# Bilinear products stored with the slice index innermost, GRU weights loaded at the start of the attention, head sums by block

## The chip, the cores and the metric
The kernel runs on one core of a Trainium2 chip. The metric is device time in microseconds of one execution: 2214.73 us is the median of three runs (2214.09 to 2214.98) of the kernel before.

## The reference
Four layers over x (4096 nodes x 128 features) and adj (4096 x 4096, sparse in values, dense in storage), each on the layer norm h of the running x. Cut to what matters here:

```python
# L0 gnn: 3 attention heads, then two GRU cells
node_support = adj_without_diagonal @ h
edge_support = mean over heads of softmax(att) * adj_without_diagonal @ (h @ W[i])
edge_output = gru(node_support, h, edge weights)
node_output = gru(edge_support, h, node weights)
x = x + diag[:, None] * (edge_output + node_output)
# L0 ffn: 1 shared + 8 routed experts, top 2
# L1 gnn (bilinear): K = 16 slices
node = h @ W1                                # 4096 x 16
hw = einsum('nc,kcf->nkf', h, W2)            # 4096 x 16 x 128
X = einsum('nk,nkf->nf', node, hw)           # sum over the 16 slices
x = x + relu(adj @ X + node @ b)
# L1 ffn: 8 routed experts, top 2
```

## The kernel before, in words
Five engines run queues of their own (SP issues all DMAs), written out by hand and tied together by counting semaphores; no planner stands behind them. The stages follow one another: layer norm, a pass over adj that counts signs and edges, softmax denominators, tables T of the heads, attention, GRU, layer norm, FFN 0, layer norm, bilinear stage, adjacency product, layer norm, FFN 1.

Attention: four blocks of 1024 output nodes (rb), each a loop over 32 tiles n of 128 adj rows. Per tile SP loads Ab (line 352) and Tt (355); GpSimd clears the diagonal where it lies in the tile (449) and raises a_prep; ScalarE makes three sigmoids ss (589) and the bf16 copy Ahi (599); VectorE makes Alo (1268), ph (1271) and pl (1274); TensorE does 24 matmuls (876) into the eight PSUM banks: heads 0 to 2 and the node support. Between blocks, after the first tile of the new block has been prepared, `evacuate` empties the banks: ScalarE copies nsT and head 2 (603, 604), VectorE multiplies each head by the reciprocal RD (1282 twice, 1285) and raises es_out. Ahead of it all SP stores the reciprocals to DRAM and waits for that store (342, 343). After the last block SP loads gruW, gruB and dB, the diagonal in every partition (366 to 368), with one semaphore g_in; GpSimd adds the three heads for all eight chunks of 512 nodes (456 to 460); VectorE (1297), TensorE (889) and GpSimd (462) wait for all three loads. VectorE then makes the bias sums gbr (1299) and releases TensorE through g_nin.

GRU: 16 groups (8 chunks, two cells s) of 12 fp32 matmuls (900 to 905), gates on ScalarE (623, 625, 630), products on VectorE (1308 to 1320), scaling by dB and the addition into xT on GpSimd (470, 474).

Bilinear stage: 32 tiles n of 128 nodes, buffers s = n % 2. TensorE makes h @ W2 for all 16 slices into four banks (12 matmuls, 986). Each slice is scaled by its node value: slices 0 to 7 by eight ScalarE copies (710), slices 8 to 15 by one VectorE product (1441). GpSimd adds the two halves of the slices (487, prod into halves), VectorE sums the remaining eight (1449, xf) and casts to bf16 (1452, Xb[0]), GpSimd makes the rest Xb[1] (493). TensorE's tile n+2 waits for the two products of n (983, 984), these for the halving of n-2 (b_half), the halving for both products of its own tile.

Of the kernel before, what the change touches and what calls it, by code (L numbers as in the profile page):

```python
# [56 lines left out]
def build(nc, a, out):  # L57
    with ExitStack() as ctx:
# [107 lines left out]
        nsT = sb("nsT", [P, N], F32, 184)  # L166
        dB = sb("dB", [P, N], F32, 104)

        gruW = sb("gruW", [P, 4, 3 * P], F32, 32)
        gruB = sb("gruB", [P, 4, 3], F32, 39)  # L170
        gbr = sb("gbr", [P, 2, 2], F32, 39.5)
        gR = [sb(f"gR{i}", [P, CH], F32, 40 + 2 * i) for i in range(2)]
        gZ = [sb(f"gZ{i}", [P, CH], F32, 44 + 2 * i) for i in range(2)]
        gM = [sb(f"gM{i}", [P, CH], F32, 48 + 2 * i) for i in range(2)]
        gU = [sb(f"gU{i}", [P, CH], F32, 52 + 2 * i) for i in range(2)]

        Wr = sb("Wr", [P, NE], F32, 56)
        rb2 = sb("rb2", [P, 2, NE], F32, 56.25)
        lg = sb("lg", [P, NT, NE], F32, 57)
        rq = sb("rq", [P, NT, NE], F32, 58)  # L180
        s1 = sb("s1", [P, NT, NE], F32, 59)
# [19 lines left out]
        bb = sb("bb", [K1, P], F32, 81.5)  # L201
        wb = sb("wb", [P, P], F32, 82)
        h3b = [sb(f"h3b{i}", [P, N], BF16, 84 + 8 * i) for i in range(2)]
        prod = [sb(f"prod{i}", [P, K1, P], F32, 100 + 8 * i) for i in range(2)]
        nodek = sb("nodek", [P, NT, K1], F32, 116)
        xf = [sb(f"xf{i}", [P, P], F32, 118 + .5 * i) for i in range(2)]
        halves = [sb(f"halves{i}", [P, K1 // 2, P], F32, 119 + 4 * i) for i in range(2)]
        Xb = [sb(f"Xb{i}", [P, NT, P], BF16, 48 + 8 * i) for i in range(2)]
        A4 = [sb(f"A4{i}", [P, N], F32, kb) for i, kb in enumerate((128, 144, 32, 64))]
        A4hi = [sb(f"A4hi{i}", [P, N], BF16, kb) for i, kb in enumerate((160, 168, 84, 92))]  # L210
# [69 lines left out]
        def _(sp):  # L280
# [82 lines left out]
            sp.wait_ge(a_lo, NRB * nsign * NT + AS)  # L363
            sp.dma_start(xT[:, :], a["xT"]).then_inc(x_in, 16)
            sp.wait_ge(es_out, HEADS * NRB + 1)
            sp.dma_start(gruW[:, :, :], a["gruW"]).then_inc(g_in, 16)
            sp.dma_start(gruB[:, :, :], a["gruB"]).then_inc(g_in, 16)
            sp.dma_start(dB[:, :], diag_d.partition_broadcast(P)).then_inc(g_in, 16)

            def ffn_loads(k, nE, nF):  # L370
                if k == 1:
# [51 lines left out]
        @block.gpsimd  # L423
        def _(pool):

            pool.wait_ge(range_l, 1)
            pool.partition_all_reduce(sm[:, 3:6], sm[:, 0:3], P, ROP.max).then_inc(range_g, 1)
            pool.wait_ge(range_l, 2)
            pool.partition_all_reduce(sm[:, 7:8], sm[:, 6:7], P, ROP.max).then_inc(range_g, 1)

            pool.wait_ge(th_hi, 1)
            pool.tensor_tensor(gwb[1][:, :], gw[:, :], gwb[0][:, :], ALU.subtract).then_inc(th_lo, 1)
            pool.wait_ge(th_hi, 2)
            pool.tensor_tensor(hTs[1][:, :], hT[:, :], hTs[0][:, :], ALU.subtract).then_inc(th_lo, 1)
            pool.wait_ge(nsign_ok, 1)
            nsign = pool.value_load(nsg[0:1, 0:1], min_val=1, max_val=2)

            for rb in range(NRB):
                with pool.Fori(0, nsign) as sg:
                    for lo, hi in ((0, rb * TPB), (rb * TPB, rb * TPB + TPB), (rb * TPB + TPB, NT)):  # L440
                        if lo == hi:
                            continue
                        with pool.Fori(lo // AS, hi // AS) as i:
                            for s in range(AS):
                                n = (rb * nsign + sg) * NT + AS * i + s
                                pool.wait_ge(a_in[s], ((rb * nsign + sg) * (NT // AS) + i) * 32 + 32)
# [8 lines left out]
            pool.wait_ge(es_out, HEADS * NRB + 1)
            for q in range(NC):
                c = slice(q * CH, (q + 1) * CH)
                pool.tensor_tensor(esT[:, c], esT[:, c], esP[:, 1, c], ALU.add).then_inc(es_add, 1)
                pool.wait_ge(es_add, q + 1)
                pool.tensor_tensor(esT[:, c], esT[:, c], esP[:, 2, c], ALU.add).then_inc(es_ok, 1)  # L460

            pool.wait_ge(g_in, 48)
            pool.wait_ge(x_in, 32)
            pool.sem_inc(g_used, 2)
            with pool.Fori(0, NC) as q:
                for s in range(2):
                    n = 2 * q + s
                    pool.wait_ge(g_new, n + 3)
                    pool.sem_inc(seen, 1)
                    pool.tensor_tensor(gU[s][:, :], gU[s][:, :], dB[:, nlast(q)], ALU.mult).then_inc(g_scaled, 1)  # L470
                    pool.wait_ge(g_scaled, n + 1)
                    pool.wait_ge(g_used, n + 2)
                    pool.sem_inc(seen, 1)
                    pool.tensor_tensor(xT[:, nlast(q)], xT[:, nlast(q)], gU[s][:, :], ALU.add).then_inc(g_used, 1)

            def bilinear_weights():
                pool.wait_ge(b_hi, 1)
                pool.tensor_tensor(bw2[1][:, :], bw2f[:, :], bw2[0][:, :], ALU.subtract).then_inc(b_w_lo, 1)
                pool.wait_ge(b_hi, 2)
                pool.tensor_tensor(bw1b[1][:, :], bw1[:, :], bw1b[0][:, :], ALU.subtract).then_inc(b_w_lo, 1)  # L480

            bilinear_weights()
            def halve(n, s):
                pool.wait_ge(b_prod_a, n + 3)
                pool.wait_ge(b_prod_d, n + 3)
                pool.wait_ge(b_sum, n + 1)
                pool.tensor_tensor(halves[s][:, :, :], prod[s][:, 0:K1 // 2, :], prod[s][:, K1 // 2:, :],  # L487
                                   ALU.add).then_inc(b_half, 1)
# [46 lines left out]
        def _(act):  # L535
# [165 lines left out]

            act.wait_ge(b_node_ok, 1)
            act.sem_inc(b_prod_a, 2)
            with act.Fori(0, NT // 2) as i:
                for s in range(2):
                    n = 2 * i + s
                    act.wait_ge(b_ps, n + 1)
                    act.wait_ge(b_half, n + 1)
                    for k in range(K1 // 2):
                        last = nc.scalar.activation(  # L710
                            prod[s][:, k, :], psum[:, 4 * s + k // 4, k % 4 * P:k % 4 * P + P], ACT.Copy,
                            scale=nodek[:, ds(n, 1), k:k + 1].rearrange("p o k -> p (o k)"))
                    last.then_inc(b_prod_a, 1)
# [46 lines left out]
        def _(pe):  # L760
# [256 lines left out]
        def _(dve):  # L1017
# [535 lines left out]
```

## Time and profile before
| | |
|---|---|
| median of 3 runs | 2214.73 us |
| profiled execution | 2213.51 us |
| its span | 2211.7 us |
| mean granted TensorE clock | 0.906 of full |
| TensorE / VectorE / ScalarE / GpSimd busy | 82% / 77% / 63% / 8% |

A row of a timeline is: start in us, duration in us, engine, line, operation, out<-in, xcount of merged instructions; in brackets how long the engine was idle before it and what released it. SPq, DVEq and the like are sequencers, PEld is TensorE's weight load.

### The profile page before, as it was taken

The page shows a single profiled execution, that of the slowest core. Times are in us where ns is not written, and L with a number is a line of the kernel's source. Part 1 is how long each engine was busy: PE and PEld are TensorE (multiplying, and loading weights), DVE is VectorE, ACT ScalarE, POOL GpSimd, SP SyncE. Part 2 cuts the span into 40 slices and gives each one's busy share as a digit, 9 for nine tenths or more (in the row PEclk, how much of TensorE's full clock was granted, in tenths as well). Part 3 has the DMA queues.
Part 4 walks back from the last instruction along what each step waited for, and adds up shares of the span by engine and source line. Part 5 has one row for each costly group of instructions (what it writes and reads, how often), then busy time and mean ns, then how long its engine had stood idle before and what let it go on. Part 6 is the DMA issues. An engine that isn't in the chain of part 4 may idle for free.

```text
span 2211.7 us, 30420 instructions
## 1 busy us (share of the span) xinstructions
PE 1821.4 (82%) x8950; PEld 875.2 (40%) x9101; DVE 1692.5 (77%) x1792; ACT 1398.9 (63%) x1767; POOL 187.9 (8%) x154
## 2 busy tenths in 40 slices
PE   4221573799999999999798899999987789997997
PEld 4111221344444444444345444444452234463332
DVE  4555427788898888888467688888859988855898
ACT  1777006778787787788334566776645567626885
POOL 0000001100000000000442000000017710000000
PEclk7555788899999999999897899999989999988999
DMA  5997025454545544554600311232030079814532
GB/s 166 429 427 319 0 80 205 162 155 150 170 150 156 169 148 154 170 151 149 238 0 0 79 38 39 48 60 45 1 123 11 0 305 429 366 39 81 98 89 76
DMA packets 79575, 313.89 MB, mean 142 GB/s; under 512 B 13958, under 2 KB 14438, under 8 KB 69494
## 3 DMA queue, kind: packets, MB, share of 16 engines
q1 hardware_dynamic: 79500, 312.98, 42.5%
q8 instruction: 36, 0.59, 0.1%
q14 instruction: 39, 0.32, 0.1%
HBM read 297.88 MB, written 15.08 MB: 142 GB/s over the span
## 4 chain that ended last, share of the span: by engine, by line
PE 40%; DVE 9%; POOL 3%; issue 3%; ACT 1%; DMA 1%; DVEq 0%; SPq 0%; POOLq 0%; ACTq 0%
PE psum L926 9%; PE psum L936 8%; PE psum L1008 7%; PE psum L876 7%; POOL halves L487 3%; DVE hidp L1382 2%; DVE xT L1404 2%; DVE yT L1401 2%; DVE prod L1441 2%; PE psum L900 1%; PE psum L902 1%; PE psum L748 1%; PE psum L914 1%; PE psum L743 1%; PE psum L754 1%
## 5 line engine op out<-in xcount | busy, mean ns | idle before, releaser
L589 ACT ACTIVATE ss<-KR,dpt 128x1024 bf16<-128x1024 int16 x384 | 413.1, 1138 | 112.0 <-DVE pl L1274 111.2
L876 PE MATMUL psum<-ph,Tt 128*128 128x512 bf16 x1502 | 411.9, 380 | 8.8 <-DVE pl L1274 7.0
L665 ACT ACTIVATE hid<-psum,fB 128x512 f32<-128x512 f32 x416 | 271.2, 686 | 151.2 <-PE psum L926 108.0
L936 PE MATMUL psum<-hidp,fW 128*128 128x512 bf16 x1215 | 289.2, 381 | 23.3 <-DVE hidp L1382 17.3
L926 PE MATMUL psum<-hTp,fW 128*128 (+1 forms) x1224 | 295.3, 384 | 5.9 <-ACT mk L679 2.8
L1382 DVE TENSOR_TENSOR hidp<-hid,hidp 128x512 bf16<-128x512 f32 x416 | 268.7, 687 | 26.7 <-DVE xT L1404 10.4
L1271 DVE TENSOR_TENSOR ph<-ss,Ahi 128x3072 bf16<-128x3072 bf16 x128 | 225.2, 1760 | 61.9 <-PE psum L876 60.2
L876 PE MATMUL psum<-pl,Tt 128*128 128x512 bf16 x752 | 225.9, 380 | 0.8
L876 PEld LDWEIGHTS psum<-ph,Tt 128*128 128x128 bf16 x1536 | 150.5, 98 | 190.4 <-issue 6.4
L1274 DVE TENSOR_TENSOR pl<-ss,Alo 128x3072 bf16<-128x3072 bf16 x128 | 224.2, 1751 | 0.0
L936 PEld LDWEIGHTS psum<-hidp,fW 128*128 128x128 bf16 x1248 | 117.6, 98 | 183.2 <-issue 42.1
L926 PEld LDWEIGHTS psum<-hTp,fW 128*128 128x128 bf16 x1248 | 123.2, 99 | 155.1 <-issue 12.1
L1268 DVE TENSOR_TENSOR Alo<-Ab,Ahi 128x1024 bf16<-128x1024 f32 x128 | 163.2, 1275 | 17.3 <-ACT Ahi L599 17.3
L876 PE MATMUL psum<-Ahi,Tt 128*128 128x512 bf16 x503 | 151.0, 380 | 24.2 <-DVE Alo L1268 20.3
L659 ACT ACTIVATE hidp<-hid 128x512 bf16<-128x512 f32 x272 | 163.4, 624 | 0.0
L1468 DVE TENSOR_TENSOR A4lo<-A,A4hi 128x4096 bf16<-128x4096 f32 x32 | 141.3, 4425 | 21.5 <-ACT A4hi L719 21.5
L541 ACT ACTIVATE Ar<-Ar 128x4096 f32<-128x4096 f32 x32 | 115.7, 3617 | 58.2 <-DVE keep L1102 58.2
L719 ACT ACTIVATE A4hi<-A 128x4096 bf16<-128x4096 f32 x32 | 115.4, 3616 | 50.0 <-PE psum L1008 23.2
L599 ACT ACTIVATE Ahi<-Ab 128x1024 bf16<-128x1024 f32 x128 | 133.3, 1042 | 6.4 <-issue 6.3
L785 PE MATMUL psum<-uvs,keep 128*128 128x18 bf16 x1024 | 32.7, 176 | 122.0 <-DVE keep L1102 122.0
L1008 PE MATMUL psum<-A4hi,Xb 128*128 128x512 bf16 x512 | 115.9, 379 | 0.0
L986 PE MATMUL psum<-bw,h3b 128*128 128x512 bf16 x368 | 86.1, 385 | 34.2 <-DVE prod L1441 32.5
(228 smaller groups left out, 2110.6 us busy)
## 6 DMA issues: line engine op xcount, KB each, us to landing
Ar<-in_adjT SPq DMA_DIRECT2D x32, 2048.0 KB, 12.9
Ab<-in_adjT SPq DMA_DIRECT2D x128, 512.0 KB, 4.1
A<-in_adjT SPq DMA_DIRECT2D x32, 2048.0 KB, 11.1
Tt<-T_d SPq DMA_DIRECT2D x128, 256.0 KB, 2.6
mB<-mk_d SPq DMA_DIRECT2D x128, 256.0 KB, 7.6
T_d<-tb SPq DMA_DIRECT2D x32, 256.0 KB, 2.0
RD<-rden_d SPq DMA_DIRECT2D x12, 512.0 KB, 5.3
fWs<-in_W SPq DMA_DIRECT2D x2, 2304.0 KB, 16.5
```

The lines of the kernel that those rows point to most:

```text
L589: last = nc.scalar.activation(ss[s % 2][:, h, :], KR[:, h, rb * RB:(rb + 1) * RB], ACT.Sigmoid, scale=STEP, bias=dpt[:, ds(t * HEADS + h, 1)])
L659: nc.scalar.activation(hidp[j % ring][:, 0, :], hid[j % HB][:, :], ACT.Copy).then_inc(hid_hi[k], 1)
L665: nc.scalar.activation(hid[j % HB][:, :], psum[:, j % HB, :], func, bias=fB1[:, j:j + 1]).then_inc(act_done[k], 1)
L876: last = nc.tensor.matmul(psum[:, 2 * h + q, :], Tt[s % AS][:, h, w, :], mv[:, q * CH:(q + 1) * CH], start=fresh and k == 0, stop=False, s ...
L926: last = nc.tensor.matmul(psum[:, j % HB, :], fW[0][x][:, j * P:(j + 1) * P], hTp[y][:, nlast(q)], start=(w == 0), stop=(w == 2))
L936: last = nc.tensor.matmul(psum[:, HB + e % dn, :], fW[1][x][:, j * P:(j + 1) * P], hidp[j % ring][:, y, :], start=(f == 0 and w == 0), sto ...
L1008: last = nc.tensor.matmul(psum[:, q, :], Xb[w][:, ds(n, 1), :].rearrange("p o f -> p (o f)"), mv[s][:, q * CH:(q + 1) * CH], start=False, ...
L1268: V.tensor_tensor(Alo[s % AS][:, :], Ab[s % AS][:, :], Ahi[s % AS][:, :], ALU.subtract).then_inc(a_lo, 1)
L1271: V.tensor_tensor(ph[s % 2][:, :, :], ss[s % 2][:, :, :], Ahi[s % AS][:, :].unsqueeze(1).to_broadcast([P, HEADS, RB]), ALU.mult).then_inc( ...
L1274: V.tensor_tensor(pl[s % 2][:, :, :], ss[s % 2][:, :, :], Alo[s % AS][:, :].unsqueeze(1).to_broadcast([P, HEADS, RB]), ALU.mult).then_inc( ...
L1382: V.tensor_tensor(hidp[j % ring][:, 1, :], hid[j % HB][:, :], hidp[j % ring][:, 0, :], ALU.subtract).then_inc(hid_lo[k], 1)
L1468: V.tensor_tensor(A4lo[s][:, :], A4[s][:, :], A4hi[s][:, :], ALU.subtract).then_inc(l_lo, 1)
```

## The change
Three edits.
1. SP issues gruW and gruB after the tables are stored and before it waits for the reciprocals; gruW, gruB, gbr, Wr and rb2 move to other addresses. dB stays behind the last evacuation and is counted on x_in, for which only GpSimd waits; TensorE waits for g_in 32 and es_out 12 instead of 48 and 13, VectorE for g_in 32.
2. GpSimd's head sums become a function for two chunks, called for block rb-1 behind the loop of block rb, and for the last block behind that.
3. prod and halves are laid out [128, 128, 16] and [128, 128, 8], the slice innermost. ScalarE's copies write one slice of it each (steps of 16 elements), VectorE's product writes through a rearranged pattern, the reduction reads contiguous memory. The cast Xb[0]<-xf goes from VectorE to ScalarE, behind the scaled copies of tile n+2.

```diff
-            sp.dma_start(gruW[:, :, :], a["gruW"]).then_inc(g_in, 16)      # behind es_out 13
-            sp.dma_start(gruB[:, :, :], a["gruB"]).then_inc(g_in, 16)
-            sp.dma_start(dB[:, :], diag_d.partition_broadcast(P)).then_inc(g_in, 16)
+            sp.dma_start(dB[:, :], diag_d.partition_broadcast(P)).then_inc(x_in, 16)
...
+            sp.dma_start(gruW[:, :, :], a["gruW"]).then_inc(g_in, 16)      # ahead of rden_ok
+            sp.dma_start(gruB[:, :, :], a["gruB"]).then_inc(g_in, 16)
             sp.wait_ge(rden_ok, 1)
...
+            def head_sums(rb):
+                pool.wait_ge(es_out, HEADS * rb + HEADS + 1)
+                for q in range(rb * RB // CH, (rb + 1) * RB // CH):
+                    c = slice(q * CH, (q + 1) * CH)
+                    pool.tensor_tensor(esT[:, c], esT[:, c], esP[:, 1, c], ALU.add).then_inc(es_add, 1)
+                    pool.wait_ge(es_add, q + 1)
+                    pool.tensor_tensor(esT[:, c], esT[:, c], esP[:, 2, c], ALU.add).then_inc(es_ok, 1)
...
+                if rb > 0:
+                    head_sums(rb - 1)
+            head_sums(NRB - 1)
+            pool.wait_ge(x_in, 48)
...
-                pool.tensor_tensor(halves[s][:, :, :], prod[s][:, 0:K1 // 2, :], prod[s][:, K1 // 2:, :],
+                pool.tensor_tensor(halves[s][:, :, :], prod[s][:, :, 0:K1 // 2], prod[s][:, :, K1 // 2:],
...
+            scaled_products(0, 0)
+            scaled_products(1, 1)
+            with act.Fori(0, NT // 2 - 1) as i:
                 for s in range(2):
+                    scaled_products(2 * i + s + 2, s)   # 8 copies into prod[s][:, :, k]
+                    high_x(2 * i + s, s)                # waits b_sum, casts xf into Xb[0]
+            high_x(NT - 2, 0)
+            high_x(NT - 1, 1)
...
-                V.tensor_tensor(prod[s][:, K1 // 2:, :],
+                V.tensor_tensor(prod[s][:, :, K1 // 2:].rearrange("p f k -> p k f"),
...
-                V.tensor_reduce(xf[s][:, :], halves[s][:, :, :].rearrange("p k f -> p f k"), AX,
-                                ALU.add).then_inc(b_sum, 1)
-                dve.wait_ge(b_sum, n + 3)
-                V.tensor_copy(Xb[0][:, ds(n, 1), :].rearrange("p o f -> p (o f)"), xf[s][:, :]).then_inc(b_x_hi, 1)
+                V.tensor_reduce(xf[s][:, :], halves[s][:, :, :], AX, ALU.add).then_inc(b_sum, 1)
```

## Rows read from the trace of the kernel before

**Rows 1.** The page's chain that ended last, by line.
```profile
PE psum L926 9%; PE psum L936 8%; PE psum L1008 7%; PE psum L876 7%; POOL halves L487 3%; DVE hidp L1382 2%; DVE xT L1404 2%; DVE yT L1401 2%; DVE prod L1441 2%; PE psum L900 1%; PE psum L902 1%; PE psum L748 1%; PE psum L914 1%; PE psum L743 1%; PE psum L754 1%
```
**Rows 2.** Timeline, from attention to GRU.
```profile
1082.80 1.22 DVE L1285 TENSOR_TENSOR esP<-esP,RD 128x1024 f32<-128x1024 f32 x1
...
1093.38 1.07 DVE L1299 TENSOR_TENSOR gbr<-gruB 128x2 f32<-128x2 f32 x2 [9.37 <-DMA dB<-diag_d]
...
1093.69 2.07 PE L900 MATMUL psum<-nsT,gruW 128*128 x2 [13.21 <-DVEq L1301]
...
1101.14 0.69 ACT L623 ACTIVATE gR<-psum,gbr 128x512 f32<-128x512 f32 x1 [18.68 <-PE psum L905]
...
1106.24 0.69 ACT L623 ACTIVATE gR<-psum,gbr 128x512 f32<-128x512 f32 x1 [3.84 <-PE psum L905]
```
**Rows 3.** A stretch: us, then PE, PEld, DVE, ACT, POOL busy (x), clock, DMA share, GB/s.
```profile
1080.00:1093.00 13.00, 0.49 (x3) 0.00 (x0) 3.49 (x3) 1.94 (x2) 8.67 (x7) 0.65 0.60 223
```
**Rows 4.** Timeline, start of the attention.
```profile
388.92 0.35 SPq L342 DMA_DIRECT2D rden_d<-den  x1
...
391.22 0.37 SPq L352 DMA_DIRECT2D Ab<-in_adjT  x1
...
399.10 1.01 PE L876 MATMUL psum<-Ahi,Tt 128*128 128x512 bf16 x2 [17.89 <-DVE Alo L1268]
```
**Rows 5.** DMA issues, 1060 to 1200: count, KB each, us to landing.
```profile
gruW<-in_gruW SPq DMA_DIRECT2D x1, 768.0 KB, 4.1
```
**Rows 6.** Timeline, VectorE and GpSimd at once in the last GRU updates.
```profile
1183.49 1.48 POOL L470 TENSOR_TENSOR gU<-gU,dB 128x512 f32<-128x512 f32 x1 [2.54 <-DVE gU L1320]
...
1183.87 1.65 DVE L1319 TENSOR_TENSOR gU<-gU,gZ 128x512 f32<-128x512 f32 x1
```
**Rows 7.** Timeline, border of attention blocks 1 and 2.
```profile
726.30 1.04 ACT L599 ACTIVATE Ahi<-Ab 128x1024 bf16<-128x1024 f32 x1
...
731.60 1.06 ACT L599 ACTIVATE Ahi<-Ab 128x1024 bf16<-128x1024 f32 x1
731.64 1.75 DVE L1274 TENSOR_TENSOR pl<-ss,Alo 128x3072 bf16<-128x3072 bf16 x1
...
740.25 2.35 DVE L1282 TENSOR_TENSOR esP<-psum,RD 128x1024 f32<-128x1024 f32 x2 [1.75 <-PE psum L876]
...
750.89 0.60 PE L876 MATMUL psum<-ph,Tt 128*128 128x512 bf16 x2 [1.87 <-DVE pl L1274]
```
**Rows 8.** Instructions grouped by line: busy us, mean ns, idle before.
```profile
L460 POOL TENSOR_TENSOR esP<-esP 128x512 f32<-128x512 f32 x8 | 10.1, 1263 | 0.6
L493 POOL TENSOR_TENSOR Xb<-xf,Xb 128x128 f32 x30 | 12.8, 426 | 8.3 <-DVE Xb L1452 8.3
L1449 DVE TENSOR_REDUCE xf<-halves 128x128 f32<-128x1024 f32 x32 | 61.7, 1928 | 0.8 <-POOL halves L487 0.8
L1353 DVE TENSOR_REDUCE rs<-rq 128x32 f32<-128x256 f32 x4 | 1.7, 420 | 0.1
L710 ACT ACTIVATE prod<-psum,nodek 128x128 f32<-128x128 f32 x256 | 69.5, 383 | 57.8 <-PE psum L986 57.8
```
**Rows 9.** Tile halves, its writer: duration ns min/median/max, first and last start.
```profile
L487 POOL TENSOR_TENSOR halves<-prod x32: 2348/2355/2364, 1657.2 to 1774.1; 128x1024 f32<-128x1024 f32 x32
```
**Rows 10.** Timeline, one beat of the bilinear stage and its last cast.
```profile
1663.70 2.35 POOL L487 TENSOR_TENSOR halves<-prod 128x1024 f32<-128x1024 f32 x1 [0.72 <-DVE prod L1441]
...
1665.47 0.67 DVE L1452 CAST Xb<-xf 128x128 f32 x1
1666.10 1.23 DVE L1441 TENSOR_TENSOR prod<-psum,nodek 128x1024 f32<-128x1024 f32 x1
...
1667.54 2.36 POOL L487 TENSOR_TENSOR halves<-prod 128x1024 f32<-128x1024 f32 x1 [0.78 <-DVE prod L1441]
...
1766.60 2.76 PE L986 MATMUL psum<-bw,h3b 128*128 128x512 bf16 x12 [1.06 <-DVE prod L1441]
...
1778.35 0.23 DVE L1452 CAST Xb<-xf 128x128 bf16<-128x128 f32 x1
```

More of the change, by code:

```diff
@@ L167, in build @@
         dB = sb("dB", [P, N], F32, 104)
-        gruW = sb("gruW", [P, 4, 3 * P], F32, 32)
-        gruB = sb("gruB", [P, 4, 3], F32, 39)
-        gbr = sb("gbr", [P, 2, 2], F32, 39.5)
+        gruW = sb("gruW", [P, 4, 3 * P], F32, 56)
+        gruB = sb("gruB", [P, 4, 3], F32, 62)
+        gbr = sb("gbr", [P, 2, 2], F32, 62.125)
         gR = [sb(f"gR{i}", [P, CH], F32, 40 + 2 * i) for i in range(2)]
@@ L175, in build @@
         gU = [sb(f"gU{i}", [P, CH], F32, 52 + 2 * i) for i in range(2)]
-        Wr = sb("Wr", [P, NE], F32, 56)
-        rb2 = sb("rb2", [P, 2, NE], F32, 56.25)
+        Wr = sb("Wr", [P, NE], F32, 62.25)
+        rb2 = sb("rb2", [P, 2, NE], F32, 62.5)
         lg = sb("lg", [P, NT, NE], F32, 57)
@@ L203, in build @@
         h3b = [sb(f"h3b{i}", [P, N], BF16, 84 + 8 * i) for i in range(2)]
-        prod = [sb(f"prod{i}", [P, K1, P], F32, 100 + 8 * i) for i in range(2)]
+        prod = [sb(f"prod{i}", [P, P, K1], F32, 100 + 8 * i) for i in range(2)]
         nodek = sb("nodek", [P, NT, K1], F32, 116)
         xf = [sb(f"xf{i}", [P, P], F32, 118 + .5 * i) for i in range(2)]
-        halves = [sb(f"halves{i}", [P, K1 // 2, P], F32, 119 + 4 * i) for i in range(2)]
+        halves = [sb(f"halves{i}", [P, P, K1 // 2], F32, 119 + 4 * i) for i in range(2)]
         Xb = [sb(f"Xb{i}", [P, NT, P], BF16, 48 + 8 * i) for i in range(2)]
@@ L452, in _ @@
                                 pool.wait_ge(a_hi, n + 1)
[L455 to L463, printed above, removed]
+                if rb > 0:
+                    head_sums(rb - 1)
+            head_sums(NRB - 1)
+            pool.wait_ge(x_in, 48)
             pool.sem_inc(g_used, 2)
@@ L703, in _, with scaled_products, high_x @@
             act.sem_inc(b_prod_a, 2)
-            with act.Fori(0, NT // 2) as i:
-                for s in range(2):
[L706 to L713, printed above, removed]
+            def scaled_products(n, s):
+                act.wait_ge(b_ps, n + 1)
+                act.wait_ge(b_half, n + 1)
+                for k in range(K1 // 2):
+                    last = nc.scalar.activation(
+                        prod[s][:, :, k], psum[:, 4 * s + k // 4, k % 4 * P:k % 4 * P + P], ACT.Copy,
+                        scale=nodek[:, ds(n, 1), k:k + 1].rearrange("p o k -> p (o k)"))
+                last.then_inc(b_prod_a, 1)
+            def high_x(n, s):
+                act.wait_ge(b_sum, n + 3)
+                nc.scalar.activation(Xb[0][:, ds(n, 1), :].rearrange("p o f -> p (o f)"), xf[s][:, :],
+                                     ACT.Copy).then_inc(b_x_hi, 1)
+            scaled_products(0, 0)
+            scaled_products(1, 1)
+            with act.Fori(0, NT // 2 - 1) as i:
+                for s in range(2):
+                    scaled_products(2 * i + s + 2, s)
+                    high_x(2 * i + s, s)
+            high_x(NT - 2, 0)
+            high_x(NT - 1, 1)
             act.wait_ge(b_x, NT + 2)
@@ L886, in _ @@
                         attend(rb, m, s)
-            pe.wait_ge(g_in, 48)
+            pe.wait_ge(g_in, 32)
             pe.wait_ge(ns_out, 2 * NRB)
-            pe.wait_ge(es_out, HEADS * NRB + 1)
+            pe.wait_ge(es_out, HEADS * NRB)
             with pe.Fori(0, NC) as q:
@@ L1295, in _ @@
             evacuate(NRB - 1)
-            dve.wait_ge(g_in, 48)
+            dve.wait_ge(g_in, 32)
             for s in range(2):
```

## The prediction
> **What bounds the kernel now.** I read the chain of waits first. By line it is TensorE for most of the span (FFN lines 926 and 936, the adjacency product 1008, attention 876), but one GpSimd line stands among them, 487, with VectorE's 1441 beside it [rows 1]: the bilinear stage is bound off TensorE. Two places then matter. In the hand-over from attention to GRU the last head is scaled at 1082.80 to 1084.02; then VectorE's little bias sum waits 9.37 us for the diagonal broadcast dB to land and TensorE stands 13.21 us until 1093.69 [rows 2]. In the bilinear stage a tile takes (1774.1 - 1657.2)/31 = 3.77 us [rows 9]. Its beat is in the timeline [rows 10]: VectorE's product ends at 1667.33, GpSimd's halving starts 0.21 later and takes 2.36, and VectorE, done with its reduction, cannot finish the bf16 cast before the halving ends: it starts at 1665.47, lasts until 1666.14 while the halving ended at 1666.05, and the same cast takes 0.23 when GpSimd is idle [last row of rows 10]. Only then does the next product start. Product 1.2 + hop 0.2 + halving 2.36 = 3.8. TensorE waits 1.06 us a tile for the product; its 12 matmuls of (2.76 - 0.38)/11 = 0.216 need 2.6.
>
> **Part 1: GRU start.** TensorE and VectorE no longer wait for dB, only for gruW and gruB, here in SBUF since the attention began. What is late next is VectorE's queue: gbr stands behind the last scaling, which ends at 1084.02, so TensorE starts at about 1084.0 instead of 1093.69: -9.7. It could be 1083.2, since at 1093 TensorE was released 0.31 after the first gbr instruction began, before the pair was done [rows 2]: VectorE's sequencer runs ahead. dB now lands some 9 us after 1084, as before; its first reader is GpSimd's scaling of the first update, which VectorE makes behind the second group's gates, and these came 1106.24 - 1093.69 = 12.5 us after TensorE's start (10 at full clock), so it stays hidden. In-block sums of the last block (4 instructions of 1.26, [rows 8]) end by 1089 and are wanted in the seventh chunk, tens of us later.
> Clock: the first group of matmuls took 1101.14 - 1093.69 = 7.4 us against 1106.24 - 1101.14 = 5.1 for the next [rows 2], because the granted clock had dropped from the 2.4 GHz level to the 1.2 GHz one: its mean over the gap is 0.65 [rows 3]. A mean of 0.65 over 1080 to 1093 at levels 1 and 0.5 puts the fall near 1084, just where TensorE will start. So between 0 and 2.2 us comes back; I take the middle, -1.1.
>
> **Part 2: the GRU loads' new place.** SP now issues gruW and gruB after the last table store and ahead of the 48 KB store of the reciprocals, whose completion gates the adjacency loads, and these TensorE's first matmul (399.10, after 17.89 us idle) [rows 4]. The store was issued at 388.92, the instant its predecessors had landed, and the first load at 391.22. Two issues of 0.35 to 0.45 come first: at least +0.8. The 768 KB transfer needs 4.1 us to land [rows 5] and goes through the same queue ahead of the store: if the store lands just behind it, the first load moves from 391.2 to about 393.4, +2.2; at most +4.3, the whole landing after both issues. I take +2.2. Attention runs at TensorE's pace from there, so nothing hides it.
>
> **Part 3: head sums by block.** Block 0 and 1's sums now stand in GpSimd's queue between two blocks: 4 instructions, and behind them the next block's a_prep, which ScalarE's Ahi needs, then Alo, ph, pl, VectorE's evacuation, and so TensorE's second head. The price depends on who has the SBUF port. At 1183.49 a GpSimd sum began, and the VectorE product begun at 1183.87 took 1.65 instead of 0.69, ending 0.55 after GpSimd [rows 6]: one waits for the whole of the other. The Trainium skill's "SBUF — State Buffer", section "SBUF: two separate sides", says just this: the port pair DVE and GpSimd share is an exclusive lock held for a whole instruction. By that rule the trace agrees, and nothing in the sum changes.
> At the border of blocks 1 and 2 GpSimd would start after Ahi at 727.3, get the port when VectorE's running instruction ends a microsecond later, and then alternate with Alo, ph and pl: 728.2 + 4 x 1.15 + the three of 1.2, 1.7 and 1.7 between them less their overlaps gives about 737.2 for the end of the fourth sum, where a_prep came at once before. Ahi moves from 731.60 to 737.3, Alo to 738.4, ph 739.6, pl 741.3, and the evacuation from 740.25 to 743.0 [rows 7]. The current block's last pl ends at 736.0 instead of 733.4 and is wanted 18 matmuls of 0.216 before the block's end at 740.1, at 736.2. TensorE's first head of the new block is 1.6 late, but on the tile behind it TensorE already waited 1.87 us for pl (at 750.89), which takes most of this up. I take +0.25 for each of two borders, +0.5; none below, and 3 each (the evacuation's delay, unabsorbed) above: 0 to +6. The sums of block 2 run beside attention's last tile, for which VectorE has finished early.
>
> **Part 4: bilinear stage.** Per tile:
> - The reduction reads contiguous memory. The same operation with the same run of eight, 256 elements, takes 0.42 [rows 8]; at 1.04 ns an element (one per VectorE cycle) 1024 take 1.21 instead of 1.93. The old one read in steps of 512 bytes, so a step costs 0.72/1024 = 0.7 ns an element on reading.
> - The product now writes in steps of 64 bytes. No strided write of that size is in the trace. Bounds: free (1.22), or twice the reading surcharge (2.65). I take the one row that shows a surcharge: 1.22 + 0.7 = 1.92. VectorE's tile is then 1.92 + 1.21 - 0.1 of overlap = 3.05.
> - ScalarE's eight copies (69.5/32 = 2.17 a tile, [rows 8]) write in the same steps: free, or 128 x 0.7 ns = 0.09 each, 2.9 for eight; twice that 3.6. I take 2.9. The cast is added: between the copies' pitch (2.17 - 0.38)/7 = 0.26 and their length 0.38, 0.3.
> - GpSimd reads two runs of eight in every sixteen and writes contiguously: I take 2.36 unchanged; bounds below.
> The tile's pace is the longest of: TensorE 2.6; VectorE 3.05; ScalarE 2.9 + 0.3 = 3.2; GpSimd 2.36 + 0.43 + 0.1 = 2.9; and the ring over two tiles, halving 2.36, hop 0.2, copies 2.9, cast 0.35, hop 0.2, split 0.43, hop 0.1 = 6.5, or 3.25 a tile. Gain (3.77 - 3.25) x 31 = -16.1.
> At the tail the last reduction is 0.65 shorter and the cast before the wb copy is gone (0.15): -0.8. The adjacency product behind it is TensorE's own and only moves; its first three tiles are loaded long before.
> The Trainium skill's "SBUF — State Buffer", section "Specifications (TRN2)", speaks against the layout: lines are 16 bytes, and each access that crosses to a new line pays unless a line is hit twice. By it the writes pay as the reads did; the case without it is the first rival. No run here shows a write yet.
>
> **The sum.** -9.7 - 1.1 + 2.2 + 0.5 - 16.1 - 0.8 = -25.0. The profiled execution took 2213.51 (span 2211.7): 2188.5. The median of the runs is 1.2 above it, so about 2189.
>
> **Rivals.**
> 1. Strided writes are free. Copies 2.17: ring 5.8/2 = 2.9, GpSimd 2.9; pace 2.95, gain 25.4, time 2189 - 9.3 = about 2180. [...] Against: the surcharge seen on reads.
> 2. Writes cost twice that. VectorE 2.65 + 1.21 - 0.1 = 3.76, ring with copies of 3.6 also 3.6: no gain in the loop, and only parts 1 to 3 and the tail (-8.9) stand: about 2206.
> 3. Slower than before: GpSimd restarts on every run of eight. Its elements cost (2.355 - 0.426)/896 = 2.15 ns [rows 8, 9]. A restart worth eight elements, 17 ns x 128 = 2.2, makes the halving 4.56 and the pace 5.1: +41 - 9 = +32, 2247. It decides from a halving of 3.5, that is a restart of 4.3 elements, where it eats the 8.9 of the other parts. For it: GpSimd is the engine next in line in the ring and has no row with short runs. Against: its plain rows scale strictly with elements.
> The Trainium skill's "GPSIMD Engine Reference", section "Performance pitfalls for Q7 kernels", gives a surcharge of half for reads whose step exceeds 8 bytes; the innermost step here is 4, so by its letter the halving stays. Counted as strided it would be 3.5, just the point where the gain is gone.
> 4. The change does not do what it says: the GRU start is held by something else (the sums, es_ok, ScalarE's evacuation). Against it: of the waits, only those for VectorE's two evacuations and ScalarE's copies can be as late as 1084, and the sums of the first blocks lie inside the attention.
>
> **Chances.** Forecast (pace 3.1 to 3.45) 0.48, its own range 2182 to 2196; rival 1 0.24; paces between the forecast and rival 2 0.15; rival 3 0.10, most of it slower; rival 4 or an attention that loses all its 6 us 0.03. The range 2175 to 2206 leaves out rival 3 and little else. Within 0.2% (4.4 us, about what a measurement of this kernel tells from no change) only a halving near 3.5 lands. Faster 0.87, same 0.03, slower 0.10.
>
> **What would show it.** The wait before the first GRU matmul at 3 to 4 us instead of 13; the first adjacency load about 4.5 us behind the reciprocals' predecessors; Alo beside GpSimd's sums at 2.3 at two borders; the reduction at 1.21, the product near 1.9, the copies' pitch near 0.35, the halving 2.36, 31 tiles 3.25 apart. Wrong if the halving is not 2.36, or if the product stays at 1.22.

## The result, and the profile after

The changed kernel takes 2176.12 us (median of four executions, 2174.39 to 2179.8) against 2214.47 (2214.09 to 2214.98) of four executions of the kernel before, taken beside it: a ratio of 0.9829, 95% interval 0.9812 to 0.9846, or 38 us less. 2189 was forecast, with a range of 2175 to 2206. The profiled execution took 2179.80 (span 2178.0, granted clock 0.906).

| stage, in the profiled executions | before | after | difference |
|---|---|---|---|
| up to the store of the last table | 388.92 | 393.14 | +4.2 |
| from there to the first attention matmul | 10.18 | 13.10 | +2.9 |
| attention | 681.43 | 680.36 | -1.1 |
| end of attention to the first layer norm matmul on xT | 97.6 | 86.8 | -10.8 |
| bilinear stage: first weight load of line 986, now 1003, to the first matmul of 997, now 1014 | 128.6 | 100.9 | -27.7 |
| all the rest | | | -1.2 |
| sum | | | -33.7 |

The first row is work that the change does not touch. Over the profiled executions of all ten kernels of this document it runs from 388.9 to 396.1, and the kernel before has the lowest. Without that row the sum is -37.9, near the 38.35 between the medians; but the profiled execution of the changed kernel was also the slowest of its four, 3.7 above their median, so the agreement is partly chance (see Open).

The chain of the page, by line, has lost GpSimd's halving (3% in [rows 1]); VectorE's product has fallen from 2% to 1%, and TensorE's own 1003 stands in their place.
```profile
PE psum L943 9%; PE psum L953 9%; PE psum L1025 8%; PE psum L893 7%; DVE hidp L1399 2%; PE psum L1003 2%; DVE xT L1421 2%; DVE yT L1418 2%; PE psum L917 1%; PE psum L919 1%; PE psum L765 1%; PE psum L931 1%; DVE prod L1458 1%; PE psum L760 1%; PE psum L771 1%
```
Timeline of the changed kernel, start of the attention (answers to [rows 4]).
```profile
393.14 0.35 SPq L341 DMA_DIRECT2D gruW<-in_gruW  x1
393.55 0.42 SPq L342 DMA_DIRECT2D gruB<-in_gruB  x1
394.01 0.43 SPq L344 DMA_DIRECT2D rden_d<-den  x1
398.57 0.35 SPq L354 DMA_DIRECT2D Ab<-in_adjT  x1
...
406.24 1.01 PE L893 MATMUL psum<-Ahi,Tt 128*128 128x512 bf16 x2 [20.82 <-DVE Alo L1285]
```
The reciprocals' store goes out 0.87 later than it could, and then needs 4.56 until the first load instead of 2.30.

Timeline from attention to GRU, and the granted clock (column 7) of the 13 us that answer to [rows 2, 3]; the whole kernel runs 6 us later here, so the stretch starts at 1086.
```profile
1086.60 2.36 DVE L1299 TENSOR_TENSOR esP<-psum,RD 128x1024 f32<-128x1024 f32 x2 [4.37 <-PE psum L893]
1088.87 1.22 DVE L1302 TENSOR_TENSOR esP<-esP,RD 128x1024 f32<-128x1024 f32 x1
1089.40 2.07 PE L917 MATMUL psum<-nsT,gruW 128*128 x2 [2.84 <-DVE esP L1299]
1090.00 0.22 DVE L1316 TENSOR_TENSOR gbr<-gruB 128x2 f32<-128x2 f32 x2
1090.11 0.33 SPq L368 DMA_DIRECT2D dB<-diag_d  x1
...
1096.37 0.69 ACT L627 ACTIVATE gR<-psum,gbr 128x512 f32<-128x512 f32 x1 [7.83 <-PE psum L922]
```
```profile
1086.00:1099.00 13.00, 10.16 (x22) 4.42 (x21) 4.84 (x7) 3.20 (x4) 5.01 (x4) 0.87 0.51 196
```
TensorE waits 2.84 us instead of 13.21, and not even for gbr: the first matmul starts at 1089.40, the bias sum at 1090.00.

Timeline of the border of blocks 1 and 2 (answers to [rows 7]): GpSimd's four sums alternate with VectorE's two-input operations, and each is stretched by the other.
```profile
733.78 1.62 POOL L442 TENSOR_TENSOR esP<-esP 128x512 f32<-128x512 f32 x1 [87.25 <-ACT Ahi L603]
734.20 2.29 DVE L1285 TENSOR_TENSOR Alo<-Ab,Ahi 128x1024 bf16<-128x1024 f32 x1
...
736.41 2.82 DVE L1288 TENSOR_TENSOR ph<-ss,Ahi 128x3072 bf16<-128x3072 bf16 x1
...
739.15 2.81 DVE L1291 TENSOR_TENSOR pl<-ss,Alo 128x3072 bf16<-128x3072 bf16 x1
...
740.43 2.66 POOL L444 TENSOR_TENSOR esP<-esP 128x512 f32<-128x512 f32 x1
...
740.89 1.06 ACT L603 ACTIVATE Ahi<-Ab 128x1024 bf16<-128x1024 f32 x1 [3.35 <-issue]
...
746.32 1.02 ACT L607 ACTIVATE nsT<-psum 128x1024 f32<-128x1024 f32 x1 [4.38 <-PE psum L893]
```
The bilinear stage: groups by line (answers to [rows 8]; busy us, mean ns, idle before), tile halves ([rows 9]), and one beat ([rows 10]).
```profile
L491 POOL TENSOR_TENSOR halves<-prod 128x1024 f32<-128x1024 f32 x32 | 75.6, 2364 | 16.3 <-ACT prod L713 15.7
L713 ACT ACTIVATE prod<-psum,nodek 128x128 f32<-128x128 f32 x256 | 73.1, 482 | 26.1 <-PE psum L1003 26.1
L1458 DVE TENSOR_TENSOR prod<-psum,nodek 128x1024 f32<-128x1024 f32 x32 | 60.7, 1897 | 5.9 <-PE psum L1003 5.9
L1466 DVE TENSOR_REDUCE xf<-halves 128x128 f32<-128x1024 f32 x32 | 38.7, 1208 | 1.9 <-POOL halves L491 1.7
L720 ACT ACTIVATE Xb<-xf 128x128 f32 (+1 forms) x32 | 11.6, 361 | 3.9 <-DVE xf L1466 3.9
```
```profile
L491 POOL TENSOR_TENSOR halves<-prod x32: 2318/2364/2377, 1652.0 to 1742.1; 128x1024 f32<-128x1024 f32 x32
```
```profile
1663.24 1.20 DVE L1466 TENSOR_REDUCE xf<-halves 128x128 f32<-128x1024 f32 x1
1663.42 2.29 ACT L713 ACTIVATE prod<-psum,nodek 128x128 f32<-128x128 f32 x8 [0.44 <-PE psum L1003]
1663.62 2.36 POOL L491 TENSOR_TENSOR halves<-prod 128x1024 f32<-128x1024 f32 x1
...
1664.35 1.91 DVE L1458 TENSOR_TENSOR prod<-psum,nodek 128x1024 f32<-128x1024 f32 x1
1665.45 0.37 ACT L720 ACTIVATE Xb<-xf 128x128 f32 x1
1666.00 0.43 POOL L497 TENSOR_TENSOR Xb<-xf,Xb 128x128 f32 x1
1666.09 1.21 DVE L1466 TENSOR_REDUCE xf<-halves 128x128 f32<-128x1024 f32 x1
1666.48 2.36 POOL L491 TENSOR_TENSOR halves<-prod 128x1024 f32<-128x1024 f32 x1
```
A tile takes (1742.1 - 1652.0)/31 = 2.91 us instead of 3.77 (the time from one tile to the next is called the pace below, GpSimd's operation on line 497 the split). No row of VectorE or GpSimd in the beat has an idle time: both have work without a break. ScalarE's eight copies still take 2.29, though each is now 0.48 long instead of 0.38.

### The profile page after: what moved, and what is told of

Same layout as the page of the kernel before. It is cut to its first block, busy times and chain, and to the rows that moved or that the text cites. A ratio compares the mean times of both kernels' runs of the same rounds, so it can differ in the third digit from the quotient of the medians.

```text
span 2178.0 us, 30551 instructions
## 1 busy us (share of the span) xinstructions
PE 1838.2 (84%) x9101; PEld 878.2 (40%) x9101; DVE 1678.1 (77%) x1760; ACT 1406.2 (65%) x1799; POOL 201.6 (9%) x154
## 4 chain that ended last, share of the span: by engine, by line
PE 43%; DVE 8%; issue 3%; ACT 1%; DMA 1%; POOL 0%; DVEq 0%; SPq 0%; ACTq 0%; POOLq 0%
PE psum L943 9%; PE psum L953 9%; PE psum L1025 8%; PE psum L893 7%; DVE hidp L1399 2%; PE psum L1003 2%; DVE xT L1421 2%; DVE yT L1418 2%; PE psum L917 1%; PE psum L919 1%; PE psum L765 1%; PE psum L931 1%; DVE prod L1458 1%; PE psum L760 1%; PE psum L771 1%
## 5 line engine op out<-in xcount | busy, mean ns | idle before, releaser
L893 PE MATMUL psum<-ph,Tt 128*128 128x512 bf16 x1536 | 416.3, 380 | 6.6 <-DVE pl L1291 6.6
L1399 DVE TENSOR_TENSOR hidp<-hid,hidp 128x512 bf16<-128x512 f32 x416 | 268.5, 687 | 27.0 <-DVE xT L1421 10.4
L1285 DVE TENSOR_TENSOR Alo<-Ab,Ahi 128x1024 bf16<-128x1024 f32 x128 | 168.0, 1312 | 18.1 <-ACT Ahi L603 18.1
L893 PEld LDWEIGHTS psum<-pl,Tt 128*128 128x128 bf16 x768 | 75.3, 98 | 91.2 <-issue 1.1
```

The costliest lines, as they stand in the source:

```text
L893: last = nc.tensor.matmul(psum[:, 2 * h + q, :], Tt[s % AS][:, h, w, :], mv[:, q * CH:(q + 1) * CH], start=fresh and k == 0, stop=False, s ...
L1285: V.tensor_tensor(Alo[s % AS][:, :], Ab[s % AS][:, :], Ahi[s % AS][:, :], ALU.subtract).then_inc(a_lo, 1)
L1399: V.tensor_tensor(hidp[j % ring][:, 1, :], hid[j % HB][:, :], hidp[j % ring][:, 0, :], ALU.subtract).then_inc(hid_lo[k], 1)
```

## The experiments

Eight kernels were run. e1 to e4 share nine executions of the kernel before (median 2215.62, 2211.98 to 2217.23), e5 to e8 nine others on another chip (2215.79, 2214.66 to 2217.61). Ratios are to these.

**e1: the cast alone.** The kernel before, with its layout, and only the cast moved to ScalarE.
```diff
                 V.tensor_reduce(xf[s][:, :], halves[s][:, :, :].rearrange("p k f -> p f k"), AX,
                                 ALU.add).then_inc(b_sum, 1)
-                dve.wait_ge(b_sum, n + 3)
-                V.tensor_copy(Xb[0][:, ds(n, 1), :].rearrange("p o f -> p (o f)"), xf[s][:, :]).then_inc(b_x_hi, 1)
...
+            def high_x(n, s):
+                act.wait_ge(b_sum, n + 3)
+                nc.scalar.activation(Xb[0][:, ds(n, 1), :].rearrange("p o f -> p (o f)"), xf[s][:, :], ACT.Copy).then_inc(b_x_hi, 1)
```


> The kernel before with one edit: the bf16 cast of the bilinear stage on ScalarE instead of VectorE, products and halves in the old layout. Theory A (the cast is what the change gained by: on VectorE it waited for GpSimd's halving, so that product, hop and halving were in series): VectorE needs 1.22 + 1.93 less 0.15 of overlap, pace 3.0 us a tile instead of 3.77, 2214.5 - 31 x 0.77 = about 2190. Theory B (the layout gained, by the shorter reduction): pace stays at 3.6 to 3.8, 2209 to 2214.

2190.17 us (2189.78 to 2194.81), ratio 0.9894 [0.9879, 0.9909]. Tile halves of e1, then its slowest line on VectorE:
```profile
L487 POOL TENSOR_TENSOR halves<-prod x32: 2347/2361/2369, 1658.8 to 1750.9; 128x1024 f32<-128x1024 f32 x32
```
```profile
L1461 DVE TENSOR_REDUCE xf<-halves 128x128 f32<-128x1024 f32 x32 | 62.6, 1956 | 1.4 <-POOL halves L487 1.4
```
Pace (1750.9 - 1658.8)/31 = 2.97. Without any new layout the stage has nearly the pace of the changed kernel: 24.8 of the 26.7 us that the pace gained.

**e2: the layout alone.** The kernel before with prod and halves laid out slice-innermost, the cast left on VectorE.
```diff
-        prod = [sb(f"prod{i}", [P, K1, P], F32, 100 + 8 * i) for i in range(2)]
+        prod = [sb(f"prod{i}", [P, P, K1], F32, 100 + 8 * i) for i in range(2)]
-        halves = [sb(f"halves{i}", [P, K1 // 2, P], F32, 119 + 4 * i) for i in range(2)]
+        halves = [sb(f"halves{i}", [P, P, K1 // 2], F32, 119 + 4 * i) for i in range(2)]
```


> The kernel before with the new layout of products and halves, the cast left on VectorE. Theory A: the series is product 1.90, hop 0.2, halving 2.36, at whose end the cast is let go, 4.46 us a tile: 2214.5 + 31 x 0.69 = about 2236, slower than before. Theory B: VectorE's own work is what counts, 1.90 + 1.21 + 0.23 instead of 1.22 + 1.93 + 0.23, about the same or faster: 2200 to 2214.

2236.24 us (2234.94 to 2237.28), ratio 1.0093 [1.0078, 1.0109]: slower than before by 21. One beat in the timeline of e2:
```profile
1664.86 1.85 DVE L1441 TENSOR_TENSOR prod<-psum,nodek 128x1024 f32<-128x1024 f32 x1
...
1666.57 1.19 DVE L1449 TENSOR_REDUCE xf<-halves 128x128 f32<-128x1024 f32 x1
1666.93 2.35 POOL L487 TENSOR_TENSOR halves<-prod 128x1024 f32<-128x1024 f32 x1 [1.37 <-DVE prod L1441]
1667.90 1.47 DVE L1451 CAST Xb<-xf 128x128 f32 x1
1669.29 1.85 DVE L1441 TENSOR_TENSOR prod<-psum,nodek 128x1024 f32<-128x1024 f32 x1
```
The reduction is done early and the cast gives that back: it lasts from 1667.90 to 1669.37, and the halving ended at 1669.28. Product 1.85, hop 0.22 (from the product's end to the halving's start) and halving 2.35 stay in series, 4.4 us, and the product in it is 0.6 longer than before.

**e3: the GRU's part alone.** The changed kernel with the bilinear stage of before (layout and cast; two places of the edit are shown).
```diff
-        prod = [sb(f"prod{i}", [P, P, K1], F32, 100 + 8 * i) for i in range(2)]
+        prod = [sb(f"prod{i}", [P, K1, P], F32, 100 + 8 * i) for i in range(2)]
...
+                dve.wait_ge(b_sum, n + 3)
+                V.tensor_copy(Xb[0][:, ds(n, 1), :].rearrange("p o f -> p (o f)"), xf[s][:, :]).then_inc(b_x_hi, 1)
```


> The GRU loads and the head sums of the change, the bilinear stage as before. If the two parts of the change are independent, the wait before the first GRU matmul falls from 13.2 to 2.8 (-10.4), the attention starts 3 later, the first group is 0.5 shorter: -8, about 2206.5, pace of the bilinear stage 3.77. If one needs the other (the clock at the FFN, say), it is off this by more than 3.

2204.10 us (2202.56 to 2206.83), ratio 0.9952 [0.9937, 0.9967]: 11.5 less. With e1's 25.4 this makes 36.9 of the 38.4; the layout's own share, on top of the cast, is the 0.06 us a tile between e1 and the changed kernel, 2 us. The expectation was 8 less and put its line at 3: it missed by 3.5. The wait and the pace came as expected (2.84, and 3.77 with the halvings from 1647.8 to 1764.7). What came on top lies in two stretches that the edit does not touch. The attention's first block took 168.3 instead of 170.9. And from the first layer norm matmul behind the GRU to the bilinear stage it took 468.8 instead of 472.1, because in that layer norm the granted clock (column 7) rose sooner. Rows of the kernel before, then of e3, both from 29.46 behind that matmul:
```profile
1207.60:1222.80 15.20, 15.20 (x87) 15.20 (x87) 10.23 (x16) 5.01 (x8) 0.00 (x0) 0.61 0.01 1
```
```profile
1201.30:1216.50 15.20, 14.26 (x97) 14.30 (x99) 10.79 (x19) 4.91 (x8) 0.00 (x0) 0.72 0.00 1
```
In the profiled executions this stretch was 468.8 to 469.4 in e3 to e8, and 471.7 to 472.1 in the kernel before, e1, e2 and the changed kernel itself. No experiment shows what decides it, and that e1 and e3 add up so closely to the whole change is partly chance.

**e4: the GRU weights loaded late.** The changed kernel, gruW and gruB issued just ahead of xT, in the attention's last microseconds and ahead of the last evacuation.
```diff
-            sp.dma_start(gruW[:, :, :], a["gruW"]).then_inc(g_in, 16)
-            sp.dma_start(gruB[:, :, :], a["gruB"]).then_inc(g_in, 16)
             sp.wait_ge(rden_ok, 1)
...
+            sp.dma_start(gruW[:, :, :], a["gruW"]).then_inc(g_in, 16)      # ahead of xT
+            sp.dma_start(gruB[:, :, :], a["gruB"]).then_inc(g_in, 16)
```


> The changed kernel, its loads of gruW and gruB moved from the start of the attention to beside the load of xT in its last microseconds. Theory: the loads delayed the store of the reciprocals and with it the attention by 3 us, and at the new place they are hidden (they land 4 to 8 us later, before the last matmul): 2176 - 3 = 2173, first adjacency load 2.3 us after the store's issue as in the kernel before, the wait before the first GRU matmul still 2.8. Rival: they land behind the 2 MB of xT's neighbours and the GRU waits for them, 2173 to 2180.

2173.18 us (2172.13 to 2177.93), ratio 0.9814 [0.9801, 0.9828]. Timeline of e4, start of the attention:
```profile
392.69 0.35 SPq L342 DMA_DIRECT2D rden_d<-den  x1
394.98 0.37 SPq L352 DMA_DIRECT2D Ab<-in_adjT  x1
...
402.94 1.01 PE L893 MATMUL psum<-Ahi,Tt 128*128 128x512 bf16 x2 [17.97 <-DVE Alo L1285]
```
First load 2.29 behind the store and first matmul 10.25, as before the change. Issued at 1071.88 the weights land in 3.9, far ahead of the 1084.49 at which TensorE wants them; the wait there stays 2.8. So the early place cost 2.9 (13.10 against 10.25 up to the first matmul) and brought nothing: what held the GRU before was dB in its counter, not gruW. The medians, 2176.12 and 2173.18, say the same, though their intervals overlap.

**e5: all head sums behind the attention.** The changed kernel, with GpSimd's 16 sums in a row, as before the change.
```diff
-                if rb > 0:
-                    head_sums(rb - 1)
-            head_sums(NRB - 1)
+            pool.wait_ge(es_out, HEADS * NRB + 1)
+            for rb in range(NRB):
+                head_sums(rb)
```


> The changed kernel with the head sums of all blocks behind the last evacuation, as before the change; loads and waits of the change stay. Theory: the sums by block neither gain nor cost: the three borders' stalls were ScalarE's slack (it waited 7.6 us for TensorE at a border before, 4.4 after), and at the end GpSimd's first chunk (2 instructions, 2.6 us) is ready before TensorE wants it, one group of 5 to 7 us after its start. 2176, within 1 us. Rival: the sums at the borders cost 1.6 us each, or the second GRU group waits for them: off by 3 us or more one way or the other.

2181.96 us (2181.01 to 2186.92), ratio 0.9854 [0.9839, 0.9869], 0.25% or some 5 us above the changed kernel's ratio (the two intervals overlap a little, so the trace has to carry it): the expectation failed, and its rival, a GRU that waits for the sums, came true, though it is the first update that waits, not the second group. Timeline of e5 in the GRU:
```profile
1106.33 1.26 POOL L444 TENSOR_TENSOR esP<-esP 128x512 f32<-128x512 f32 x1
1106.52 1.62 DVE L1334 TENSOR_TENSOR gU<-hT,gM 128x512 f32<-128x512 f32 x1 [5.18 <-POOLq L467]
...
1112.60 1.12 PE L916 MATMUL psum<-nsT,gruW 128*128 x2 [3.77 <-DVE gM L1327]
1113.56 1.44 PE L918 MATMUL psum<-hT,gruW 128*128 x2
```
The sums keep GpSimd from 1087.03 to 1107.59, VectorE's update waits 5.18 for it, and TensorE 3.77 for VectorE; its next matmuls are slow again (8 of them in 1117.83 - 1112.60 = 5.2 instead of 3.4). From the end of the attention to the first layer norm matmul e5 takes 1176.2 - 1083.46 = 92.7 against 86.8, 5.9 more. The time from one evacuation to the next is the same with the sums between the blocks, without them, and before the change: 170.2, 170.1 and 170.1. (Of the three sets of sums inside the attention two stand between blocks, the third beside the last tile; the expectation counts three borders.)

**e6: GpSimd turns the layout.** The changed kernel with contiguous products; the halving writes slice-innermost.
```diff
-                pool.tensor_tensor(halves[s][:, :, :], prod[s][:, :, 0:K1 // 2], prod[s][:, :, K1 // 2:],
+                pool.tensor_tensor(halves[s][:, :, :].rearrange("p f k -> p k f"),
+                                   prod[s][:, 0:K1 // 2, :], prod[s][:, K1 // 2:, :],
...
-                V.tensor_tensor(prod[s][:, :, K1 // 2:].rearrange("p f k -> p k f"),
+                V.tensor_tensor(prod[s][:, K1 // 2:, :],
```


> The changed kernel with products stored contiguously as before the change; GpSimd reads them contiguously and writes the halves slice-innermost (steps of 32 bytes); the reduction stays contiguous. VectorE needs 1.22 + 1.21 less 0.2 = 2.25 a tile instead of 2.9. Theory A (GpSimd bounds the tile: halving 2.36, gap 0.13, split 0.43 = 2.92, and a strided write costs it nothing): pace 2.9 as in the changed kernel, about 2176. Theory B (VectorE bounds it): pace 2.7, 2170. Rival C (GpSimd pays for strided writes what VectorE does, 0.66 ns an element): halving 3.03, pace 3.6, 2198.

2176.26 us (2175.00 to 2176.85), ratio 0.9820 [0.9805, 0.9835]. Tile halves of e6 and its product:
```profile
L491 POOL TENSOR_TENSOR halves<-prod x32: 2372/2382/2397, 1651.2 to 1738.3; 128x1024 f32<-128x1024 f32 x32
```
```profile
L1458 DVE TENSOR_TENSOR prod<-psum,nodek 128x1024 f32<-128x1024 f32 x32 | 38.9, 1215 | 6.9 <-PE psum L1003 6.9
```
GpSimd writes with steps of 32 bytes for 0.02 us; VectorE's product is back at 1.22, its tile at 2.44 of 2.81. GpSimd's own (2.38 + 0.43) now makes the pace: between the theories' 2.9 and 2.7, for A's reason. The gain of 0.10 us a tile is 3 us in the trace and lost in the spread of the times.

**e7: one split for all tiles.** The changed kernel with late weights, xf kept for all 32 tiles, and Xb[1] made by one VectorE subtraction behind the loop.
```diff
-                pool.tensor_tensor(Xb[1][:, ds(n, 1), :].rearrange("p o f -> p (o f)"), xf[s][:, :], hi, ALU.subtract).then_inc(b_x, 1)
...
+            V.tensor_tensor(Xb[1][:, :, :], xfa[:, :, :], Xb[0][:, :, :], ALU.subtract).then_inc(b_x, 1)
```


> The kernel with the late load, and GpSimd without the 32 splits: the sums xf of all tiles are kept and VectorE makes the low parts in one instruction of 4.4 us behind the last tile, beside TensorE's fp32 matmuls of node @ b. GpSimd then needs 2.36 a tile. Theory B (VectorE, 1.90 + 1.21 less overlap, bounds the changed kernel too): pace stays at 2.87 to 2.9, 2173. Theory A (GpSimd bounds alone): pace falls to 2.65 to 2.7, 2165.

2176.06 us (2174.61 to 2179.77), ratio 0.9823 [0.9808, 0.9838]. Tile halves of e7:
```profile
L491 POOL TENSOR_TENSOR halves<-prod x32: 2317/2364/2376, 1647.1 to 1736.2; 128x1024 f32<-128x1024 f32 x32
```
Pace 2.87 with GpSimd down to 2.36 a tile: VectorE alone (1.90 + 1.21, less the overlap) holds it there too. The time is 3 us above the expected 2173 (e4's). The intervals of the two ratios overlap, and the profiled execution lost against e4's 2.8 in the attention's first block and 2.1 behind the start of the adjacency product (425.4 against 423.3; e8, with the same late split, takes 422.8 there).

**e8: both reliefs.** e7 with e6's layout.
```diff
-        prod = [sb(f"prod{i}", [P, P, K1], F32, 100 + 8 * i) for i in range(2)]
+        prod = [sb(f"prod{i}", [P, K1, P], F32, 100 + 8 * i) for i in range(2)]
...
+                pool.tensor_tensor(halves[s][:, :, :].rearrange("p f k -> p k f"),
+                                   prod[s][:, 0:K1 // 2, :], prod[s][:, K1 // 2:, :],
```

> Both: no splits on GpSimd, contiguous products, GpSimd turning the halves, with the late load. If VectorE and GpSimd are level in the changed kernel, only this frees both: VectorE 2.25, GpSimd 2.36, ScalarE 2.55, TensorE 12 x 0.216 = 2.6: pace 2.65, 2173 - 0.25 x 31 = about 2165. Rival C (GpSimd's strided write costs 0.66 ns an element): halving 3.03, pace 3.1, 2179.

2164.05 us (2162.77 to 2167.22), ratio 0.9768 [0.9755, 0.9782]: the best of all, 12 us below the changed kernel, of which the late load has 3 (e4). 2165 was expected. Tile halves, 20 matmuls (a tile has 12) without a gap, and the end of the stage, where the one split of 4.43 costs TensorE 0.56:
```profile
L491 POOL TENSOR_TENSOR halves<-prod x32: 2369/2382/2392, 1645.2 to 1726.5; 128x1024 f32<-128x1024 f32 x32
```
```profile
1651.65 4.54 PE L994 MATMUL psum<-bw,h3b 128*128 128x512 bf16 x20
```
```profile
1730.55 4.43 DVE L1471 TENSOR_TENSOR Xb<-xfa,Xb 128x4096 bf16<-128x4096 f32 x1 [0.25 <-ACT Xb L710]
...
1739.94 1.90 PE L1017 MATMUL psum<-A4hi,Xb 128*128 128x512 bf16 x8 [0.56 <-DVE A4lo L1477]
```
The pace is 2.62, TensorE's own 12 x 0.216. e6 and e7 each took one of two equal bounds away, to 2.81 and 2.87; only both together reach the third.

## Why the prediction was right, and where it was not

**Direction and place** were right: e3 and e1 show the two parts that it named as the gain. The size was not: 38 us less, where 25 were forecast. 2176.12 lies 1.1 us inside the lower end of a range 31 us wide, below the 2182 to 2196 of the forecast's own mechanism and below rival 1's 2180, so it is the width of the range that holds it. The sum itself has small slips: 2188.5 + 1.2 is 2189.7, not 2189; a pace of 3.1 gives 2185, not 2182; the tail's reduction is 0.72 shorter, not 0.65.

**Part 4, the term that was mis-sized.** Product 1.92 forecast, 1.90 measured; reduction 1.21 and 1.21; halving 2.36 and 2.36. The failed step is "ScalarE's eight copies write in the same steps: free, or 128 x 0.7 ns = 0.09 each, 2.9 for eight; I take 2.9". A copy did get 0.1 longer (383 to 482 ns on average), but the next starts before it ends, and the pitch from copy to copy hardly moved: 2.17 for eight became 2.28. The surcharge was put on the pitch and landed on the length. With 2.28 the ring is 2.36 + 0.2 + 2.28 + 0.35 + 0.2 + 0.43 + 0.1 = 5.9, or 2.96 a tile, and ScalarE's tile is 2.6. A second, smaller miss is VectorE's overlap: product and reduction of 1.90 and 1.21 follow each other in 1666.09 - 1663.24 = 2.85, so they overlap by 0.26, not 0.1, and VectorE's tile is not 3.05. What is left as the longest are VectorE and GpSimd (1666.48 - 1663.62 = 2.86), over all tiles 2.91: -26.7 instead of -16.1. e6, e7 and e8 bear this out. The pace is nearly rival 1's 2.95 (given 0.24), its condition, that strided writes are free, only half true: the writes cost ScalarE no pace, and VectorE (1897 - 1218)/1024 = 0.66 ns an element at the step of 64 bytes.

The Trainium skill's "SBUF — State Buffer", section "Specifications (TRN2)", gives one rule and names no engine: each access that crosses to a new line of 16 bytes pays. VectorE's writes bear it out (1.22 to 1.90); GpSimd's do not (2.36 to 2.38 at steps of 32 bytes in e6), nor does the pitch of ScalarE's copies.

**Which edit earned it** the prediction left unsaid. It described the block rightly (VectorE's cast waits for GpSimd's halving, so product and halving run in series), yet worked the gain out from all edits together. e1 and e2 separate them: the cast is the gain, and the layout, which fills most of the diff, costs 21 us without it. Of VectorE's operations in the stage only the cast was stretched by the halving: 0.67 and 1.47 us instead of the 0.23 of [rows 10]. The product reads PSUM and nodek, the reduction halves alone, and both kept their lengths beside a running halving (product 1.24 on average in e1, reduction 1.93 in [rows 8]). That fits the Trainium skill's "VectorE: DVE Perf Modes", section "What auto-detection actually checks", by which a single-source operation whose source and destination lie in SBUF runs in the mode 2x_2P if its outermost dimension is even, together with the lock that the prediction names. That this is the cast's mode no run here shows by itself; that the cast ends only with the halving, the rows show.

**Part 1.** -9.7 forecast; the wait shrank from 13.21 to 2.84, 10.4, since the sequencer of VectorE had let TensorE go before the bias sum ran, the 0.8 that the text named as possible. The clock gave less: the first group took 6.97 (1096.37 - 1089.40) instead of 7.45, 0.5 of the 1.1. The mean over 13 us rose from 0.65 to 0.87, but behind the wait of 2.84 the first two matmuls still took 2.07, the 1.2 GHz level, as before. In e5, behind the same wait, they took 1.66. Whether a shorter wait would keep the 2.4 GHz level was not tried.

**Part 2.** +2.2 forecast, +2.9 measured, within its bounds. e4 shows it as the whole cost of the place.

**Part 3.** The stretched operations came as described (Alo 2.29, ph and pl 2.8). Ahi at 740.89 is 3.2 late by the clock of the kernel before (the block ends at 746.32 instead of 740.25), where 5.7 was forecast: it was released 0.46 behind the start of the last sum, at 740.43, not behind its end. The attention absorbed all of it: 0 instead of +0.5 (170.2 from evacuation to evacuation in both). ScalarE had waited 7.6 us before the evacuation and now waits 4.38. What the prediction missed is the other end: it priced this edit at a cost only, while without it part 1 would lose nearly 6 of its 10 us (e5). In the kernel before, the 16 sums were hidden behind dB. These rows of it show the last sum, and the first update 4.3 us behind its end:
```profile
1103.36 1.27 POOL L460 TENSOR_TENSOR esP<-esP 128x512 f32<-128x512 f32 x1
...
1108.93 0.69 DVE L1318 TENSOR_TENSOR gU<-hT,gM 128x512 f32<-128x512 f32 x1
```
Once TensorE starts 10 us sooner, the sums are what is late. The rule "where a stall goes, say what is late next" was followed for TensorE's and VectorE's queues, not for GpSimd's.

**The tail.** -0.8 forecast; from the last halving's start to the first matmul behind the stage it is 3.8 (1742.12 to 1745.95) instead of 4.8 (1774.06 to 1778.83).

**The rivals.** 2 is out by the product's 1.90, 3 by the halving's 2.36, 4 by the 2.84.

**Open.** Three stretches that no edit touches differ between profiled executions: the stages up to the attention (388.9 to 396.1); the attention's first block, 168.3 (e3 to e6), 169.9 (changed kernel) and 170.8 to 171.0 (kernel before, e1, e2, e7, e8), with the moment at which the granted clock rises; and the stretch from the layer norm behind the GRU to the bilinear stage (e3), some 3 us shorter in the six experiments that have the GRU's part. The prediction has no term for any of them. Whether the GRU's part earned those 3 us is not shown: the one profiled execution of the changed kernel does not have them, and it was its slowest.

## What to carry to other kernels

When one engine's small operation waits for another engine's long one, move the small one before touching the long one's layout: here 32 casts of 0.23 us alone (0.67 as they stood) were worth 25 us, and the layout without that move cost 21. A gain from removing a stall has to be priced with every queue that the stall was hiding, and a term with two equal bounds gives nothing until both are lifted. A surcharge on an operation's length is a surcharge on the pace only where the operations do not overlap.

## What the hardware showed that was not expected

- The same strided write costs three engines differently: VectorE 0.68 us on 1024 elements, ScalarE 0.10 of length and about 0.01 of pitch on 128, GpSimd 0.02 on 1024.
- GpSimd's two-input sum of 1.26 us took 1.62 to 2.77 beside VectorE's two-input operations, and these grew by up to 1.1 us each.
- A 48 KB store issued 0.9 us behind a 768 KB load delayed the next step by 2.3 us more than alone (4.56 against 2.29).
